# A selective scan with a mixture of experts on one core: the first decay ahead of the router's copies, unread products on TensorE in the prologue, z's gates a step later, expert rows loaded a tile ahead

## The reference

```
xn = layernorm(x)
# s: one Mamba mixer and one small MLP, both with a residual
h  = rmsnorm(xn); xp, z = split(h @ in_proj.T)            # 512 channels each
xc = silu(conv4(xp) + conv_b)                             # causal, 4 taps, per channel
dt, B, C = split(xc @ x_proj.T)                           # 16, 16, 16
dt = softplus(dt @ dt_proj.T + dt_b)
state[t] = state[t-1] * exp(dt * A) + dt * xc * B[t]      # 512 channels x 16 states
y  = sum over states (state * C) + xc * D
s1 = xn + (y * silu(z)) @ out_proj.T
s  = s1 + silu(rmsnorm(s1) @ mlp_w1.T) @ mlp_w2.T
# g: 8 experts with a hidden size of 1024, top 2 of a softmax router
g  = silu(sum over top 2 (gate_e * (relu(xn @ w1_e + b1_e) @ w2_e + b2_e)))
out = x + s * g
```

## Time and profile before

| | us |
|---|---|
| median of 3 runs (lowest, highest) | 1527.77 (1526.65, 1530.67) |
| the profiled execution | 1529.59 |
| its span, first to last instruction | 1527.8 |

### The profile page before, as it was taken

One profiled execution on the slowest core, in us unless ns is written; L12 is line 12 of the kernel. 1 busy time (PEld: TensorE's weight loads), 2 busy tenths in 40 slices (PEclk: granted clock), 3 DMA queues, 4 the chain that ended last, 5 costly groups with the idle time before them and its releaser, 6 DMA issues.

```text
span 1527.8 us, 17205 instructions
## 1 busy us (share of the span) xinstructions
PE 1257.8 (82%) x4966; PEld 915.4 (60%) x4966; DVE 1241.7 (81%) x1547; ACT 897.9 (59%) x1972; POOL 1202.9 (79%) x638
## 2 busy tenths in 40 slices
PE   3875473689879988979898997989898998889977
PEld 2642121577667756767676766766686676655546
DVE  6599875599878987798888997799889897977844
ACT  4542453476757756675767765676767475645432
POOL 0444888798898878897799889797999799986830
PEclk8586887799999989999999999999999999979989
DMA  4773543688597757876597758786789569456640
GB/s 170 252 286 132 158 159 117 234 247 251 153 317 227 229 149 223 281 226 224 160 310 237 238 153 275 251 247 194 225 300 271 191 190 326 150 194 204 216 133 28
DMA packets 131518, 325.79 MB, mean 213 GB/s; under 512 B 15176, under 2 KB 29904, under 8 KB 120928
## 3 DMA queue, kind: packets, MB, share of 16 engines
q1 hardware_dynamic: 112224, 272.91, 52.8%
q0 software_dynamic: 13056, 41.95, 11.9%
q10 hardware_dynamic: 6144, 9.83, 1.8%
HBM read 259.75 MB, written 39.71 MB: 196 GB/s over the span
## 4 chain that ended last, share of the span: by engine, by line
PE 42%; DVE 13%; issue 10%; DMA 8%; POOL 8%; ACT 7%; SPq 1%; DVEq 0%; ACTq 0%; POOLq 0%
PE prod L1030 37%; DVE state L1415 9%; DMA xs<-slot_x 7%; POOL slot_x L732 4%; POOL dbu L745 3%; PE prod L1035 2%; ACT state L832 1%; PE prod L1217 1%; DVE prod L1453 1%; PE prod L1218 1%; DVE hxc L1383 1%; DVE late L1480 1%; POOL late L803 1%; PE prod L1082 1%; ACT late L996 1%
## 5 line engine op out<-in xcount | busy, mean ns | idle before, releaser
L1415 DVE TENSOR_TENSOR_SCAN state<-state,carry,dbu 128x512 f32<-128x512 f32 x512 | 657.3, 1284 | 126.3 <-ACT state L832 87.2
L745 POOL TENSOR_TENSOR dbu<-dtu,bb 128x1024 f32<-128x1024 f32 x256 | 630.5, 2468 | 58.3 <-DVE state L1415 50.5
L756 POOL TENSOR_TENSOR hxc<-hxc 128x1024 f32<-128x1024 f32 x155 | 376.9, 2432 | 117.7 <-DVE hxc L1383 117.6
L1383 DVE TENSOR_TENSOR hxc<-state,cb 128x512 f32<-128x512 f32 x512 | 353.6, 691 | 38.9 <-DVE state L1415 1.9
L832 ACT ACTIVATE state<-dt,par 128x512 f32<-128x512 f32 x512 | 352.6, 692 | 52.9 <-DVE hxc L1383 38.0
L1030 PE MATMUL prod<-xsT,late 128*128 128x256 f32 (+1 forms) x1280 | 269.9, 366 | 23.2 <-issue 9.9
L1030 PE MATMUL prod<-late 128*128 128x256 f32 x1136 | 274.2, 399 | 13.2 <-issue 11.7
L1030 PEld LDWEIGHTS prod<-xsT,late 128*128 128x128 f32 x1280 | 226.4, 196 | 70.1 <-issue 31.9
L1030 PEld LDWEIGHTS prod<-late 128*128 128x128 f32 x1136 | 231.9, 207 | 50.6 <-issue 21.9
L1082 PE MATMUL prod<-hxc,ident 128*128 128x512 f32 x212 | 122.2, 708 | 63.6 <-DVE hxc L1383 57.2
L830 ACT COPY carry<-state 128x1 f32<-128x1 f32 x384 | 60.9, 158 | 162.3 <-DVE hxc L1383 154.3
(11 more groups left out here) (168 smaller groups left out, 1254.2 us busy)
## 6 DMA issues: line engine op xcount, KB each, us to landing
bb<-bc_rows SPq DMA_DIRECT2D x256, 256.0 KB, 5.8
cb<-bc_rows SPq DMA_DIRECT2D x256, 256.0 KB, 4.9
late<-moe SPq DMA_DIRECT2D x40, 1028.0 KB, 5.3
late<-moe SPq DMA_DIRECT2D x40, 1024.0 KB, 6.5
hxc<-hxc POOLq DMA_DIRECT2D x36, 512.0 KB, 7.2
slot_x<-xc SPq DMA_DIRECT2D x18, 512.0 KB, 5.8
xs<-slot_x SPq DMA_DIRECT2D x31, 256.0 KB, 6.7
slot_y<-ys ACTq DMA_DIRECT2D x31, 256.0 KB, 5.3
```

What stands on the lines that cost most here:

```text
L745: nc.gpsimd.tensor_tensor(dbu[:, v % 3, :, :], dtu[:, n % 2, 2 * h:2 * h + 2, :], b, ALU.mult).then_inc(dbu_ready, 1)
L756: nc.gpsimd.tensor_tensor(hxc[:, to, :, :], hxc[:, to, :, :], hxc[:, piece, :, :], ALU.add).then_inc(summed, 1)
L1383: nc.vector.tensor_tensor(hxc[:, buf, c, :], state[:, k % STATES, :], cb[:, v % 4, :], ALU.mult).then_inc(hc_ready, 1)
L1415: nc.vector.tensor_tensor_scan(state[:, k % STATES, :], state[:, k % STATES, :], dbu[:, v % 3, c, :], carry[:, n % 2, col(k):col(k) + 1], ...
```

## The change

Four edits. (1) In `FIRST`, SPE and SPL stand ahead of the copies TX10 and TX11, and ACT's first decay stands ahead of TX20; it is no longer behind the whole list. PE's own order stays as it was. (2) PE runs 10 products before it waits for the parameters, 4 ahead of LG0, 8 ahead of XD and 2 ahead of LG2. Each is 128x128 by 128x512 from constants, into the third `state` bank, and nobody reads the result. (3) On DVE z's gates stand two steps later than their slot, where it was one. Since `bank_uses` looks at the reader's step, banks can be dealt out otherwise. (4) SP loads the rows of tile i+2 at MT of tile i, ahead of the wait for the last UP and of `w1`, once the transposes of tile i, which read the same half of `xs`, are done; it no longer does so at NEXT.

```diff
@@ -66,8 +66,9 @@
            "M110": 107, "M111": 109, "M112": 111, "M113": 114, "M210": 117, "M211": 119, "STORE": 121}
 FIRST = """A.LOADX A.XR A.TR0 A.TR1 R.TX00 R.TX01 L.L1 L.L2 A.IN0 A.IN1 A.CV0a A.CV0b A.CV0c A.TH0 L.L3 A.IN2
  A.CV1a A.CV1b A.CV1c A.TH1 A.SL0 A.IN3 R.LG0 L.L4 A.CV2a A.CV2b A.CV2c A.TH2 A.SL1 L.L5 A.CV3a A.CV3b A.CV3c A.TH3 A.SL2 A.SL3
- L.L6 L.L7 L.ROOT L.XN A.XD A.BOUT A.DT0 A.DT1 A.DT2 A.DT3 R.TX10 R.TX11 R.LG1 A.SPE A.SPL R.TX20 R.TX21 R.LG2
+ L.L6 L.L7 L.ROOT L.XN A.XD A.BOUT A.DT0 A.DT1 A.DT2 A.DT3 A.SPE A.SPL R.TX10 R.TX11 R.LG1 S.FIRST R.TX20 R.TX21 R.LG2
  R.TX30 R.TX31 R.LG3 A.DTA0 A.DTU0 A.DTA1 A.DTU1"""
+WARM = {"start": 10, "LG0": 4, "XD": 8, "LG2": 2}
 R_AT = 13
 R_FIRST = 4
 M_ORDER = sorted(range(TILES), key=lambda i: (i + 0.5) / PAIRS if i < PAIRS else (i - PAIRS + 0.5) / (TILES - PAIRS))
@@ -92,7 +93,7 @@
 
 VECTOR_WORK = ("RO", "CV", "SL", "YE", "Z0", "Z1", "Z2", "Z3", "OU", "RC", "M1", "AD", "FI")
 BETWEEN = ("CV", "YE", "OU", "M2")
-LATER = {"act": {"R": 1, "M": 1, "C": 1, "A": 2}, "dve": {"M": 1, "C": 1, "A": 0}, "pool": {"Y": 1, "A": 1},
+LATER = {"act": {"R": 1, "M": 1, "C": 1, "A": 2}, "dve": {"M": 1, "C": 1, "A": 0, "Z0": 2, "Z1": 2, "Z2": 2, "Z3": 2}, "pool": {"Y": 1, "A": 1},
          "pe": {"Y": 4}, "sp": {"M": 2}}
 
 
@@ -576,7 +577,6 @@
         def walk(engine, do):
             for kind, name, i in PROLOGUE:
                 do(kind, name, i)
-            do("S", "FIRST", None)
             for kind, name, i in program(engine):
                 do(kind, name, i)
 
@@ -685,13 +685,17 @@
                     sp.dma_start(out_t[i // 2, i % 2], sx[i % 2][:, 0]).then_inc(stored[i % 2], 16)
                 elif kind == "M":
                     if name == "MT" and i < TILES - 1:
+                        if i < TILES - 2:
+                            if i:
+                                full(sp, ("M", "MT", i - 1))
+                            else:
+                                full(sp, ("M", "START", 1))
+                            load_rows(i + 2)
                         read_out(sp, ("M", "UP%d" % (2 * size(i) - 1), i))
                         load_first(i + 1)
                     elif name == "NEXT" and i < TILES - 1:
                         full(sp, ("M", "DN0", i))
                         load_second(i + 1)
-                        if i < TILES - 2:
-                            load_rows(i + 2)
 
             walk("sp", do)
             for b in range(2):
@@ -1022,8 +1026,14 @@
 
         @block.tensor
         def _(pe):
+            def warm(n):
+
+                for k in range(n):
+                    pe.matmul(state[:, STATES - 1, :], ident[:, :], zeros[:, 0:BT], start=True, stop=True)
+
+            pe.wait_ge(consts, CONSTS)
+            warm(WARM["start"])
             pe.wait_ge(params_in, 64)
-            pe.wait_ge(consts, CONSTS)
 
             def products(dst, lhs, rhs, n):
                 for k in range(n):
@@ -1037,6 +1047,8 @@
 
             def do(kind, name, i):
                 key = (kind, name, i)
+                if name in WARM and not i:
+                    warm(WARM[name])
                 if kind == "A" and key in USES:
                     p = i % 2
                     dst = bank(key)
```

## The result

The changed kernel takes 1508.41 us (median of 4 runs, 1497.09 to 1509.8), the kernel before 1529.22 us (median of 4, 1526.65 to 1543.23) in the same session. The medians are 20.8 us apart, which is 1.4%. The ratio estimated from these runs is 0.9841, with a 95% interval of 0.9803 to 0.9879: 1.6% faster, or 24 us. The quotient of the medians, 0.9864, lies inside that interval. The profiled execution of the changed kernel took 1507.25 us, its span is 1505.5.

A forecast was written before the change was run, and what follows sets the result against it. It took PE's products to hold the end most, with DVE at z's first gates in six of eight blocks. Prologue +1, rows -9, gates -8, banks 0 made -16 us on 1529.6, or 1513.6; median 1512 us, range 1495 to 1531.

The forecast's parts named there:

- The queue to `w1` (rival b): Experts' stretch: rows ahead of `w1` delay it, +17 in place of -9, 1538 us; its own chance is not stated.
- the gates' term: z's first gates on DVE: a scan fits inside the tanh wait, 2.0 us in four blocks, -8 us (-12 to +4).
- the rows': Experts' stretch: all 14 waits at MT go, `w2` is late next; -9 us (-45 to +17).
- the prologue's: Prologue up to the first scans: later start and second scan, partly given back; +1 us (-3 to +6).
- the sum behind the size: Rows at 14 tiles: gains up to `w2`'s landing, 20.8 us, capped by `w1`'s slack to 12.5, then less 2 and 1.5.
- the 0.5 that I allowed: Experts' stretch: landings of `w1` (L597) would be longer by less than 0.5 us on the median.
- in two of them PE then waits for the bank, and the gain is given back: z's second gate: it frees its bank later, so two of six blocks lose their 2.0 us.
- the sign I had named: DVE's waits for z's tanh would fall from 37 to below 10 us, with no new ones before the scans.
- the last two gates are slack: Third gate of a block: its waits of 1.6 to 3.8 us lie where PE holds the end, giving DVE only slack.
- the new banks are by themselves worth nothing: Banks dealt out otherwise: no price in the trace, put at 0 with 5 us to either side.
- Rival (d): Prologue: the second scan is late by 6 us and no stall gives it back; 1517 us, chance 0.10.
- The stall of 1.4 us at 85 to 89 us: End of the prologue: faster PE would remove ACT's stall, which cost DVE 1.4 us.

The follow-up runs named there:

- experiment 3: The kernel before with only the prologue's new order and unread products: 1530.38 us, ratio 1.0035.
- experiment 2: The kernel before with only the rows of an expert tile loaded a tile ahead: 1519.36 us, ratio 0.9953.
- experiment 1: The kernel before with only z's gates a step later on DVE and the banks that follow from it: 1508.76 us, ratio 0.9888.
- Experiment 7: The changed kernel with only the first half of each `w2` loaded from the second tile on: 1503.46 us, ratio 0.9835 to the kernel before.
- experiment 6: The changed kernel with banks dealt out by the read steps of the kernel before: 1510.87 us, ratio 0.9887 to the kernel before.
- experiment 9: The kernel before with only the first two gates of each block (Z0, Z1) a step later: 1508.96 us, ratio 0.9897.
- 10, last two gates: The kernel before with only the third and fourth gate of each block (Z2, Z3) a step later: 1528.14 us, ratio 1.0014.
- 4, banks: The kernel before with z's gates unmoved but banks dealt out as if they stood a step later: 1529.12 us, ratio 1.0021.
- 5, gates and rows: The kernel before with z's gates a step later and rows a tile ahead, prologue unedited: 1499.62 us, ratio 0.9809.
- 8, rows behind `w1`: The changed kernel with the rows issued at the same MT but behind `w1`: 1502.41 us, ratio 0.9837 to the kernel before.
- 12, none at the start: The changed kernel without the 10 unread products at the start, the other 14 kept: 1507.61 us, ratio 0.9876 to the kernel before.
- experiment 11: The changed kernel without any unread products, new prologue order kept: 1500.99 us, ratio 0.9847 to the kernel before.

## Why the prediction was right, and where it was not

The forecast was 1512 us; 1508.41 came. The signs hold, that of the prologue too, and the queue to `w1` decides nothing, as forecast. The sizes do not hold as well as the total. Alone the edits make +5.3 (experiment 3), -7.2 (2) and -17.1 us (1), -19 together, against -24 by the ratio for all (-21 by the medians); the intervals leave that difference open. The forecast had +1, -9 and -8, together -16. So the gates' term was 9 us too small, and the rows' and the prologue's were 2 and 4 us too good. That the total came out 3.6 us from the measured median is in good part luck: errors of opposite sign cancelled.

**Rows: the mechanism held, and the size, -7.2 against -9.** The 14 waits at MT went, `w2` of the same tile was late next in 12 places, and DN0 began at its landing. But the trace does not bear out the sum behind the size. I added PE's time tile by tile as if each microsecond were one of the whole, and expected about 25 us of waits for `w2`; 38.8 came at DN0. Experiment 7 took away 23 us of the waits for weights for nothing. That -9 came out near -7.2 has a reason in part, since the sum kept only what the next wait left over, and is luck in part. The interval of experiment 2 (3 to 11 us) can't tell the two figures apart.

**The queue to `w1` (rival b)** is refuted: with the rows behind `w1` the time is the same. `w1`'s landing is 0.6 us longer on the median than before (5.3 in the earlier trace rows, 5.9 after), a little over the 0.5 that I allowed, `w2`'s 0.5 (6.5 to 7.0).

**The gates: the failed step is "in two of them PE then waits for the bank, and the gain is given back".** The term was -8 us; alone the edit gave -17. The 2.0 us a block are right, but I took four blocks. The trace of experiment 1 has the step in all eight, and that of experiment 6, with the old banks and the wait of 3.22 us still there, as well (3.7 us in the very block of that wait). What I read as a give-back was a wait of PE with the scans not behind it: the bank was late for PE, and the scans went on all the same. Nor was the chain through the first gate, which I found in six blocks, a guide to how many of them gain. Eight steps of 2.0 us make 16, and experiment 9's ratio makes 15.7 (1.03% of 1524.4). DVE's waits for z's tanh fell from 37.4 us (16 times) to 5.2 us (7) over the whole execution, as the sign I had named asks, and from 28.9 (11) to 3.7 us (4) between 270 and 1300 us. That the last two gates are slack, and that the new banks are by themselves worth nothing, held (experiments 10 and 4).

**Prologue.** The +1.4 us of the changed kernel's profile looks like the +1 of the forecast, but it is one execution against one. The start of scan 16 in all profiles, us:

| | scan 16 |
|---|---|
| prologue as before (before, 1, 2, 4, 5, 9, 10) | 108.1, 108.2, 107.4, 106.8, 107.2, 106.6, 107.2; mean 107.4 |
| prologue of the change (changed, 3, 6, 7, 8) | 109.5, 110.9, 112.3, 112.1, 109.8; mean 110.9 |

So the new prologue costs about 3.6 us at scan 16, which fits experiment 3 (+5.3), and the profile of before was one of the late ones of its kind. The term was too small. DVE's wait for the second decay is one part of it (4.08 us in the change). The clock may be another: in experiments 6 and 7, which are the latest, XD took 5.30 us and DT 5.08 and 5.23, in the change 3.61 and 4.20.

In the change's own profile the first convolution moved by 1.86 us (19.39 to 21.25), inside 0.4 to 2.1, beyond the 1.2 taken. XD took 3.61 us instead of 6.51 and nothing came of it, for the reason given: the square root at 43.95 stands ahead of its copy at 44.10 (forecast 43.6). The first scan came at 63.79 (64.4 forecast); the second at 69.96, not at 72.2. I had priced the two unread products ahead of LG2 at up to 3.5 us, they took 2.56, and behind them LG2 and TX3 took 1.85 and 1.07. Rival (d), a second scan 6 us late, is refuted: it came 0.1 us late in the change, and 1.4 at most with this prologue. The ten products at the start ended between 14.8 and 16.3 us in the five kernels that have them, where I had 14.3 to 16.0. The stall of 1.4 us at 85 to 89 us, which I expected to be given back, stayed: DVE waits 2.05 us for ACT at 88.08 and 90.47, and scans 16 to 64 are 1.4 us late throughout.

**What the prediction did not have at all** is the clock in the experts' stretch. Of 23.7 us won there, 17.0 are PE's products going faster and 6.7 idle time. The same measure over the same scans for other kernels (length of the stretch; PE's busy time; the rest of it; time at 1.2 GHz, summed over slices of 2 us):

| | length | PE busy | PE idle | at 1.2 GHz |
|---|---|---|---|---|
| before | 1001.2 | 882.9 | 118.3 | 105 |
| 10, last two gates | 1000.3 | 880.4 | 119.9 | 102 |
| 4, banks | 999.7 | 880.9 | 118.9 | 98 |
| 3, prologue | 999.2 | 881.7 | 117.5 | 105 |
| 9, first two gates | 990.7 | 878.9 | 111.8 | 102 |
| 2, rows | 987.4 | 878.8 | 108.6 | 95 |
| 1, gates | 982.1 | 875.0 | 107.1 | 88 |
| 7, half of `w2` | 980.5 | 875.5 | 105.0 | 81 |
| changed | 977.5 | 866.0 | 111.6 | 61 |
| 12, none at the start | 976.9 | 872.3 | 104.6 | 74 |
| 6, old banks | 976.7 | 867.1 | 109.6 | 70 |
| 5, gates and rows | 975.0 | 868.1 | 107.0 | 64 |
| 11, no unread products | 973.6 | 870.9 | 102.7 | 70 |
| 8, rows behind `w1` | 971.6 | 867.6 | 104.0 | 64 |

With gates and rows both, the time at 1.2 GHz lies between 61 and 81 us and PE's busy time between 866.0 and 875.5; with neither (before, 3, 4) they are 98 to 105 and 880.9 to 882.9. The change has the lowest of the seven, so the 17.0 us of faster products are the most that any profile shows.

The place of the earlier trace rows shows how a wait and the clock can go together. Before, the clock fell behind the wait of 3.23 us; the eight products at 568.64 took 3.69 us, and 12.8 us went from 564.08 to the transposes at 576.87:

```profile
566.64 2.07 PE L1067 MATMUL prod<-xdT,wdt 16*128 16x512 f32 x2
568.64 3.69 PE L1030 MATMUL prod<-xsT,late 128*128 128x256 f32 x8
```

After, there is no such wait, the clock stays full, and the same sequence goes from 558.02 to 567.90, 9.9 us with a wait of 0.31 in it:

```profile
558.02 1.99 PE L1040 MATMUL prod<-xsT,late 128*128 128x256 f32 x8
559.95 1.12 PE L1079 MATMUL prod<-xdT,wdt 16*128 16x512 f32 x2
561.37 1.99 PE L1040 MATMUL prod<-xsT,late 128*128 128x256 f32 x8 [0.31 <-DVE xc L1474]
```

Experiment 6 has the wait of 3.22 us and yet kept the full clock, and its same sequence took 9.5 us, from 563.74 to 573.25. So a wait of PE can cost about its own length again in slower products, and need not. Whether the faster products made the kernel faster, or the kernel with fewer stalls merely shows a higher clock, was not separated: no kernel held the clock and kept the waits. Three things speak against the clock as the main cause. The two orders differ: the change has the least time at 1.2 GHz, not the shortest stretch. Experiment 9 stood at 1.2 GHz for 102 us, nearly as long as before, and still gained 15.7 us. And the mean granted clock of whole executions does not order their times: the change ran 1507.25 us at 0.931 and 1497.09 at 0.930, and experiment 11 six times at 0.912 to 0.918, in 1500.61 to 1505.85 us.

Open: why the changed kernel's four runs (1497.09 to 1509.8) spread by 0.8%, which the clock does not explain, and whether the edits together give more than their sum.

## What to carry to other kernels

A wait that ends at a transfer is worth only the distance to what is late next; read that landing for each place before counting the wait. A wait counts where the engine that sets the pace stands behind it: moving DVE's gate behind one scan gained its 2.0 us in every block, while 23 us fewer waits of PE for weights gained nothing, most of them having become other waits. Compare kernels by the starts of an operation that both run in one order, and compare the busy time of the same work too, since it changes with the granted clock. One profile of each kernel is not enough for a term of a few microseconds: the change's prologue cost 1.4 us in one pair of profiles, and 3.6 us on the mean of all.

## What the runs showed of the hardware

- **The clock does not fall after every wait of the same length.** Before, PE waited 3.23 us at 564.08, and the eight products took 2.63 us, then 3.69. In experiment 6 it waited 3.22 us at the same place of the program, and the eight took 1.99.
- **Unread products did not make the clock certain.** Ten of them from 4.39 on took 11.73 us in the change, 10.46 in experiment 3, 11.16, 11.02 and 11.92 in 6, 7 and 8: so the products took their shorter time from another moment on in each. (The granted clock of the windows can't show this: it reads 1.00 from the start of the trace, with PE still idle.) XD, with eight unread products ahead of it, took 3.60 to 3.61 us in the change and in experiments 8 and 12, and 5.30 in 3, 6 and 7. DT's eight products, 16 rows deep, took 5.17 us before; 4.20, 3.69, 5.08, 5.23 and 4.04 in the change and in 3, 6, 7 and 8; 6.51 in 12, and 3.69 in 11, which has no unread products at all.
- **With nothing but transposes (products with the identity) ahead, PE reached its full speed.** In the earlier trace rows eight take 1.94 us at 12.87, as they do at a granted clock of 0.5 (1.95 at 63.20). The next eight, the router's, took less, and the input products behind them, at 16.04, took 0.88 us a product, the time that the prediction has for full clock; after the unread products eight transposes take 1.04. PE's timeline of before:

```profile
14.60 1.60 PE L1035 MATMUL prod<-ident,late 128*128 128x128 f32 x8
```

- **A transfer of half the size does not land in half the time.** Under the load of this stretch 1 MB took 7.0 us from issue to landing (the change) and 0.5 MB 5.5 us (experiment 7; medians of `w2`'s loads).
